# A graph-attention kernel whose GpSimd engine waits for finished sums at every fourth group of gathered rows instead of at every group

## The chip, the cores and the metric

The kernel runs on one core of a Trainium2 chip. The metric is the time of one execution on the device in microseconds (us). TensorE (PE) multiplies matrices, VectorE (DVE) and ScalarE (ACT) work elementwise, GpSimd (POOL) issues the gathers of rows, and SyncE (SP) issues the plain DMA transfers. The engines run their own instruction streams and meet at semaphores only.

## What is computed

A graph of 3,125 nodes with 256 features each goes through one layer: a layer norm, then x + graph attention + linear attention, then a second layer norm and a mixture of eight experts, of which every node uses two. The part that matters here is the graph attention over 53,125 edges (50,000 and a loop for each node), sorted by destination:

```
h = (x @ W).reshape(n, HEADS, C)
logits = a_src[src] + a_dst[dst]
logits = jnp.where(logits >= 0, logits, NEG_SLOPE * logits)
ex = jnp.exp(logits - seg_max[dst])
alpha = ex / (denom[dst] + 1e-16)
msgs = alpha[:, :, None] * h[src]
out = jax.ops.segment_sum(msgs, dst, num_segments=n)
```

The row `h[src]` of every edge has to be fetched from memory by an index, weighted, and added to the row of its destination.

## The kernel before

**Stages.** First all nodes are normalised and projected, and a table `h_table` with a row of 260 float32 for each node (256 features and 4 source logits) is written to memory. Then comes the edge loop, in which the linear attention and the second layer norm are worked in at fixed steps, and last the experts. The edges stand in 416 tiles of 128. Four tiles are a group (`G = 4`), so there are 104 groups (`NGRP`), numbered 0 to 103. The edge loop is written out group by group for every engine; on the inputs here it runs once.

**The ring.** The buffer `gathered` has eight places (`RING = 8`), and group `s` uses place `s % 8`. For each group GpSimd issues four indirect DMAs (L567), one for each tile: 128 rows of `h_table` picked by `src_row`. Place `r` may be overwritten once the sum that read it is finished. The semaphore `summed` says so: it starts at 8 and TensorE adds 1 at the end of each group's sum, so that the wait for `s + 1` before group `s` is a wait for the sum of group `s - 8`.

**A group's way.** TensorE spreads the destination's logits over the edges (`spread`, four products at L830, with some side work of `chain`: L855, L856, L861) and signals `ad_ready`. It does so three groups ahead. VectorE waits for the gather and for `ad_ready`, both before one instruction (`logits` part 0, L1161), finishes the logits (L1164, L1168), ScalarE takes the exponential (L681, L690), and VectorE weights the rows (`weigh`, L1173). TensorE then multiplies the rows by a one-hot matrix (the sum, four products at L887) and signals `summed`. VectorE adds the result to `acc` (`add_sums`, L1148). In the order of VectorE's code `weigh(n)` stands ahead of `logits(n + 2, part 0)`, and in TensorE's `spread(n + 3)` and `chain` stand ahead of the sum of group `n`:

```
                        if ahead >= 3:
                            last = spread(n + 3, s + 3, (r + 3) % RING)
                            last = chain(c, s + 3, last)
                            last.then_inc(ad_ready, 1)
                        pe.wait_ge(weighted, n + 1)
```

The trace has two matmul records for each float32 product, so 8 records at L887 are one group's sum and 8 at L830 one group's spread.

GpSimd does nothing else in this loop but wait, count and issue gathers. Two of its groups have another wait besides: group 3 for the copied keys and group 6 for the copied values of the linear attention.

Of the kernel before, what the change touches and what calls it, by code (L numbers as in the profile page):

```python
# [48 lines left out]
RING = 8  # L49
NGRP = ET // G  # L50
# [19 lines left out]
SLACK = 11  # L70
KGRP = -(-NT // G)
PLACES = 4
FAR = 3e38
EPS = 1e-5
SLOPE = 0.2
# [65 lines left out]
def graph_layer(nc, x, src, dst, w_gat, att_src, att_dst, gat_bias, w_qkv, w_out, b_out,  # L141
# [5 lines left out]
    with ExitStack() as whole:  # L147
        def sem(name):
            return whole.enter_context(nc.semaphore(name))
# [42 lines left out]
        waited = sem("waited")  # L192
# [6 lines left out]
        with ExitStack() as scope:  # L199
# [197 lines left out]
            summed = sem("summed")  # L397
# [15 lines left out]
            with nc.Block() as block:  # L413
# [86 lines left out]
                def _(pool):  # L500
# [54 lines left out]
                    with pool.Fori(0, passes) as c:  # L555
                        for s in range(NGRP):
                            r = s % RING

                            pool.wait_ge(summed, c * NGRP + s + 1)
                            pool.sem_inc(waited, 1)  # L560
                            if s == 3:
                                pool.wait_ge(k_copied, KGRP)
                            if s == 6:
                                pool.wait_ge(v_copied, KGRP)
                            for j in range(G):
                                t = s * G + j
                                pool.indirect_dma_start(gathered[:, r, j, :], None, h_table,  # L567
                                                        bass.IndirectOffsetOnAxis(ap=src_row[:, t:t + 1], axis=0)
                                                        ).then_inc(gather_done[r], 16)
# [794 lines left out]
        with ExitStack() as scope:  # L1364
# [13 lines left out]
            place, in_tile, what = [], [], []  # L1378
            for k in range(PLACES):
                at = k * sum(sizes)  # L1380
# [38 lines left out]
            with nc.Block() as block:  # L1419
# [26 lines left out]
                def _(pool):  # L1446
                    pool.memset(zeros[:, :], 0.0).then_inc(zeros_ready, 1)
                    for m in range(NCHOICE // UNROLL):
# [3 lines left out]
                        grid = (P, UNROLL, UT)  # L1452
                        pool.tensor_tensor(what[m % PLACES][:, :, 0, :], in_tile[m % PLACES],
                                           node_id[:, nodes].unsqueeze(2).broadcast_to(grid), ALU.mult).then_inc(what_ready, 1)

                @block.scalar
                def _(act):
                    act.wait_ge(ratio_ready, 1)
                    act.activation(ratio[:, :], ratio[:, :], ACT.Exp).then_inc(exp2_ready, 1)
                    for m in range(NCHOICE // UNROLL):  # L1460
                        act.wait_ge(tiles_found, m + 1)
                        for k in range(UNROLL):
                            n = m * UNROLL + k
                            op = act.activation(what[m % PLACES][:, k, 1, :], in_tile[m % PLACES][:, k, :], ACT.Copy,
                                                scale=share[:, n // NT, n % NT:n % NT + 1])
# [3 lines left out]
                def _(pe):  # L1469
# [11 lines left out]
                    for n in range(NCHOICE):  # L1481
# [3 lines left out]
                        m, k = n // UNROLL, n % UNROLL  # L1485
                        pe.matmul(bank[3][:, 0:2 * UT], place[m % PLACES][:, k, :],
                                  what[m % PLACES][:, k, :, :].rearrange("p a b -> p (a b)"),
                                  start=(n == 0), stop=(n == NCHOICE - 1)).then_inc(placed, 1)

                @block.vector  # L1490
                def _(dve):
                    def after(instruction):
                        v3.done(instruction)
                        dve.wait_ge(v3.sem, v3.n)
# [7 lines left out]
                    def choose(k):  # L1502

                        after(dve.tensor_reduce(best[:, k, :], gate[:, :, :], AX.X, ALU.max))
                        after(dve.tensor_tensor(ranked[:, :, :], gate[:, :, :], best[:, k, :].unsqueeze(2).broadcast_to(each), ALU.is_equal))
                        after(dve.tensor_tensor(ranked[:, :, :], ranked[:, :, :], by_rank, ALU.mult))
                        after(dve.tensor_reduce(first_rank[:, k, :], ranked[:, :, :], AX.X, ALU.max))
                        after(dve.tensor_tensor(choice[:, k * NT:(k + 1) * NT, :], by_rank,
                                                first_rank[:, k, :].unsqueeze(2).broadcast_to(each), ALU.is_equal))

                    choose(0)
                    after(dve.scalar_tensor_tensor(out=gate[:, :, :], in0=choice[:, 0:NT, :], scalar=-FAR, in1=gate[:, :, :],
                                                   op0=ALU.mult, op1=ALU.add))
# [34 lines left out]
                    def find(m):  # L1548
                        if m >= PLACES:

                            dve.wait_ge(placed, (m - PLACES + 1) * UNROLL)
                        some = slice(m * UNROLL, (m + 1) * UNROLL)
                        grid = (P, UNROLL, UT)
                        dve.tensor_tensor(in_tile[m % PLACES], tile_no[:, :].unsqueeze(1).broadcast_to(grid),
                                          slot_at[:, 1, some].unsqueeze(2).broadcast_to(grid), ALU.is_equal).then_inc(tiles_found, 1)
                        dve.tensor_tensor(place[m % PLACES], iota_row[:, :].unsqueeze(1).broadcast_to((P, UNROLL, P)),
                                          slot_at[:, 0, some].unsqueeze(2).broadcast_to((P, UNROLL, P)), ALU.is_equal).then_inc(places_ready, 1)
# [236 lines left out]
```

## Time and profile before

| what | value |
|---|---|
| median of 3 runs | 1165.52 us (1161.57 to 1167.33) |
| the profiled execution | 1165.62 us, span 1163.3 us |
| PE busy | 946.3 us, 81% of the span |
| DVE busy | 491.5 us, 42% |
| ACT busy | 397.3 us, 34% |
| POOL busy | 552.8 us, 48% |
| mean granted TensorE clock | 0.839 of full speed |

The profile is of one execution. Shares of busy time are averages over stages with different limits: the edge loop ends at about 708 us, and the rest of the span belongs to the experts. A PE record has a modelled end. An idle time in brackets is that of the engine just ahead of the instruction, with what ended it; "remote" is a semaphore whose sender the profile doesn't name, "issue" is no wait that the profile shows.

### The profile page before, as it was taken

What the parts mean: (1) busy time and instruction counts of PE and PEld (TensorE: products, weight loads), DVE (VectorE), ACT (ScalarE), POOL (GpSimd) and SP (SyncE); (2) the same over time, 40 slices, a digit from 0 to 9 for tenths busy, and PEclk for the clock granted to TensorE, in tenths of its full rate; (3) what the DMA queues carried; (4) which work ended last, traced back from release to release, by engine and by line L of the source; (5) the groups of instructions that cost most, each with busy time, mean ns of one, the idle gap of its engine ahead of it and who ended that gap; (6) DMA issues with size and microseconds to landing.
All of it is one profiled execution on the core that took longest, in us unless ns stands there. A gap on an engine that the chain in (4) does not pass through costs nothing. (4 is left out here: it accounts for less than half of the span.)

```text
span 1163.3 us, 18718 instructions
## 1 busy us (share of the span) xinstructions
PE 946.3 (81%) x5176; PEld 826.4 (71%) x5177; DVE 491.5 (42%) x1352; ACT 397.3 (34%) x1098; POOL 552.8 (48%) x572
## 2 busy tenths in 40 slices
PE   6949678687797888577568385599999999999995
PEld 5848656566675667466457373599999999999994
DVE  5754464555465466547457366711111111111110
ACT  4516332324233333333433222443333333333331
POOL 2263666666666666666566620423333333333332
PEclk8986977776877777777667677799999999999998
DMA  7342443444434444445444423956665655665661
GB/s 196 105 114 82 116 112 104 119 111 128 137 112 123 137 110 126 133 112 140 126 112 110 128 65 125 330 168 177 178 179 164 180 169 177 180 178 179 180 181 19
DMA packets 76350, 163.54 MB, mean 141 GB/s; under 512 B 11520, under 2 KB 40725, under 8 KB 76163
## 3 DMA queue, kind: packets, MB, share of 16 engines
q0 software_dynamic: 30144, 69.30, 24.7%
q1 hardware_dynamic: 45587, 93.02, 23.8%
q10 hardware_dynamic: 560, 0.52, 0.2%
q8 instruction: 25, 0.41, 0.1%
q14 instruction: 34, 0.28, 0.1%
HBM read 145.82 MB, written 16.99 MB: 140 GB/s over the span
## 5 line engine op out<-in xcount | busy, mean ns | idle before, releaser
L567 POOL DMA_INDIRECT gathered<-h_table,src_row x416 | 396.6, 953 | 233.6 <-issue 120.1
L887 PE MATMUL bank<-gathered,one_hot 128*128 128x260 f32 x832 | 281.3, 490 | 74.0 <-issue 43.1
L887 PEld LDWEIGHTS bank<-gathered,one_hot 128*128 128x128 f32 x832 | 192.3, 243 | 125.3 <-issue 90.2
L1676 ACT ACTIVATE hiddenT<-bank,b_slot 128x128 f32<-128x128 f32 x424 | 120.8, 368 | 248.6 <-PE bank L1711 248.5
L1654 POOL DMA_INDIRECT out<-y,add_index x53 | 84.4, 1593 | 248.2 <-DVE y L1766 122.5
L1711 PEld LDWEIGHTS bank<-xgT,acc 128*128 128x128 f32 x1696 | 198.5, 193 | 2.6
L1711 PE MATMUL bank<-xgT,acc 128*128 128x128 f32 x1696 | 198.7, 276 | 0.0
L1729 PE MATMUL bank<-w_sb,hiddenT 128*128 x848 | 193.2, 381 | 0.0
L830 PEld LDWEIGHTS bank<-adc,w_sb 128*128 128x128 f32 x832 | 138.7, 232 | 62.8 <-issue 52.2
L1729 PEld LDWEIGHTS bank<-w_sb,hiddenT 128*128 128x128 f32 x848 | 157.0, 190 | 21.7 <-issue 1.7
L830 PE MATMUL bank<-adc,w_sb 128*128 x832 | 123.0, 268 | 50.1 <-issue 49.8
L681 ACT ACTIVATE bank<-z 128x16 f32<-128x16 f32 x104 | 19.4, 187 | 390.4 <-DVE z L1168 339.7
L1173 DVE TENSOR_TENSOR gathered<-gathered,bank 128x1024 f32<-128x1024 f32 x104 | 126.1, 1213 | 0.9 <-ACT gathered L690 0.8
L1763 DVE CAST add_index<-slot_token 128x1 uint32 (+1 forms) x53 | 8.1, 154 | 279.6 <-PE bank L1729 279.6
L1161 DVE TENSOR_TENSOR z<-gathered,bank 128x16 f32<-128x16 f32 x104 | 17.4, 167 | 232.7 <-remote 201.5
L1148 DVE TENSOR_TENSOR acc<-acc,bank 64x260 f32 x208 | 87.8, 422 | 28.0 <-issue 23.1
L659 ACT ACTIVATE w_sb<-w_sb,minus_lane 128x512 f32<-128x512 int16 x104 | 74.8, 719 | 12.2 <-ACT w_sb L664 2.7
L664 ACT ACTIVATE w_sb<-w_sb,ones 128x512 f32<-128x512 f32 x104 | 73.7, 708 | 3.0 <-PE bank L830 2.7
L1136 DVE TENSOR_TENSOR one_hot<-bank,beyond 128x512 f32<-128x512 f32 x104 | 70.8, 684 | 0.4 <-issue 0.2
L1642 POOL DMA_INDIRECT xg<-xn_table,read_index x53 | 52.2, 985 | 22.4 <-issue 15.8
L855 PE MATMUL bank<-w_mix,xnT 128*128 128x256 f32 x100 | 36.9, 491 | 6.6 <-issue 6.4
L781 PE MATMUL bank<-w_sb,xnT 128*128 128x128 f32 x200 | 27.9, 303 | 7.1 <-ACT w_sb L621 5.6
(238 smaller groups left out, 697.1 us busy)
## 6 DMA issues: line engine op xcount, KB each, us to landing
acc<-in_L_ffn_W SPq DMA_DIRECT2D x53, 1024.0 KB
w_sb<-key_table SPq DMA_DIRECT2D x52, 256.0 KB
w_sb<-in_L_ffn_W SPq DMA_DIRECT2D x8, 1024.0 KB, 12.4
gathered<-h_table,src_row POOLq DMA_INDIRECT x416
h_table<-acc SPq DMA_DIRECT2D x25, 130.0 KB, 2.0
out<-w_sb SPq DMA_DIRECT2D x5, 512.0 KB
xn_table<-w_sb SPq DMA_DIRECT2D x5, 512.0 KB
xs<-in_x SPq DMA_DIRECT2D x3, 640.0 KB, 10.9
```

The costliest lines, as they stand in the source:

```text
L567: pool.indirect_dma_start(gathered[:, r, j, :], None, h_table, bass.IndirectOffsetOnAxis(ap=src_row[:, t:t + 1], axis=0)).then_inc(gather_ ...
L659: act.activation(key_offs, keys[:, q % KEYS, s % KBLK, :], ACT.Abs, bias=minus_lane[:, :]).then_inc(key_off, 1)
L664: act.activation(one_hotT[:, r % HOTS, :, :].rearrange("p a b -> p (a b)"), key_offs, ACT.Relu, bias=ones[:, 0:1], scale=-1.0).then_inc(ho ...
L830: mm = pe.matmul(ad_bank[r % ADS][:, j * 2 * HEADS:(j + 1) * 2 * HEADS], one_hotT[:, r % HOTS, j, :], flat(adc[:, bass.ds(k, 1), :]), star ...
L887: mm = pe.matmul(sum_bank[r % SUMS][:, 0:ROW], one_hot[:, r, j, :], gathered[:, r, j, :], start=(j == 0), stop=(j == G - 1))
L1136: dve.tensor_tensor(one_hot[:, r, :, :], lanes(place).unsqueeze(1).broadcast_to((P, G, P)), local[:, bass.ds(s * G, G)].unsqueeze(2).broad ...
L1148: dve.tensor_tensor(total, total, sum_bank[r % SUMS][part_of, 0:ROW], ALU.add).then_inc(added, 1)
L1173: dve.tensor_tensor(message, message, alpha(r).unsqueeze(3).broadcast_to((P, G, HEADS, C)), ALU.mult).then_inc(weighted, 1)
L1654: pool.indirect_dma_start(out, bass.IndirectOffsetOnAxis(ap=add_index[:, k:k + 1], axis=0), y[:, k, :], None, compute_op=ALU.add).then_inc ...
L1676: op = act.activation(hiddenT[:, k, g * P:(g + 1) * P], bank[1 + 2 * k + half][:, f * P:(f + 1) * P], ACT.Gelu, bias=b1_slot[:, k, g:g + 1])
L1711: mm = pe.matmul(bank[1 + 2 * k + f // 4][:, f % 4 * P:(f % 4 + 1) * P], w1_slot[:, k, c, f * P:(f + 1) * P], xgT[:, k, c * P:(c + 1) * P] ...
L1729: mm = pe.matmul(bank[5 + k][:, 0:D], hiddenT[:, k, f * P:(f + 1) * P], flat(w2_sb[:, bass.ds(e * KF + f, 1), :]), start=(f == 0), stop=(f ...
```

## The change

GpSimd no longer waits before each group. It waits before groups 0, 4, 8 and so on, and there for the sums of four groups at once: before group `s` for `s + 4`, which is for all sums up to that of group `s - 5`. It then issues the 16 gathers of groups `s` to `s + 3` with no wait for a sum between them. The count `waited` is raised as often as there are such waits. The other engines, the ring, and the gathers themselves are as before.

```diff
+HALF_RING = RING // 2
...
                         for s in range(NGRP):
                             r = s % RING
 
-                            pool.wait_ge(summed, c * NGRP + s + 1)
-                            pool.sem_inc(waited, 1)
+                            if s % HALF_RING == 0:
+                                pool.wait_ge(summed, c * NGRP + s + HALF_RING)
+                                pool.sem_inc(waited, 1)
                             if s == 3:
                                 pool.wait_ge(k_copied, KGRP)
```

In the instruction list of GpSimd, in the edge loop past group 7, the kernel before has a wait for `summed` at each fourth gather (the register operation is part of the loop's counting):

```order
L567 DMA gathered<-h_table,src_row 128x260 [waits summed]
L567 DMA gathered<-h_table,src_row 128x260 x3
L559 REGISTER_ALU
L567 DMA gathered<-h_table,src_row 128x260 [waits summed]
L567 DMA gathered<-h_table,src_row 128x260 x3
L559 REGISTER_ALU
```

At the same place of the changed kernel, where the gather's line is L569, and from group 4 on:

```order
L569 DMA gathered<-h_table,src_row 128x260 [waits summed]
L569 DMA gathered<-h_table,src_row 128x260 x7
L569 DMA gathered<-h_table,src_row 128x260 [waits v_copied]
L569 DMA gathered<-h_table,src_row 128x260 x7
L561 REGISTER_ALU
L569 DMA gathered<-h_table,src_row 128x260 [waits summed]
L569 DMA gathered<-h_table,src_row 128x260 x15
```

No gather has moved against another; what changes is that 16 of them now stand between two waits.

## Rows read from the trace of the kernel before

**Rows 1.** The page: the span, and the costliest groups of the edge loop

```profile
span 1163.3 us, 18718 instructions
...
L567 POOL DMA_INDIRECT gathered<-h_table,src_row x416 | 396.6, 953 | 233.6 <-issue 120.1
...
L1161 DVE TENSOR_TENSOR z<-gathered,bank 128x16 f32<-128x16 f32 x104 | 17.4, 167 | 232.7 <-remote 201.5
```

**Rows 2.** Windows, L887 alone: stretch, length, PE and PEld busy (count), PEclk, DMA, GB/s

```profile
52.00:125.00 73.00, 12.61 (x38) 9.34 (x39) 0.77 0.36 100
125.00:680.00 555.00, 254.82 (x747) 173.26 (x745) 0.75 0.44 121
680.00:708.50 28.50, 13.88 (x48) 9.72 (x48) 0.88 0.08 26
```

**Rows 3.** Line L567 by itself: ns of one, first and last start, idle before

```profile
L567 POOL DMA_INDIRECT gathered<-h_table,src_row x416: 940/946/1848, 51.8 to 678.7; - x139
...
  remote: 73.8, 23
  PE bank L887: 28.6, 11
```

**Rows 4.** Timeline 391 to 416 us: start, us busy, instruction, idle before

```profile
391.68 0.94 POOL L567 DMA_INDIRECT gathered<-h_table,src_row  x1 [3.17 <-PE bank L887]
...
400.63 0.41 PE L861 MATMUL bank<-ident,w_sb 128*128 128x128 f32 x2
...
400.88 1.92 PE L887 MATMUL bank<-gathered,one_hot 128*128 128x260 f32 x8
...
405.43 0.95 POOL L567 DMA_INDIRECT gathered<-h_table,src_row  x1 [0.30 <-issue]
...
408.75 0.17 DVE L1161 TENSOR_TENSOR z<-gathered,bank 128x16 f32<-128x16 f32 x1 [8.14 <-remote]
...
409.53 0.95 POOL L567 DMA_INDIRECT gathered<-h_table,src_row  x1 [3.15 <-PE bank L887]
...
412.15 3.83 PE L887 MATMUL bank<-gathered,one_hot 128*128 128x260 f32 x8 [2.06 <-DVE gathered L1173]
```

**Rows 5.** Groups by line, everything up to 402.9 us: counts

```profile
L567 POOL DMA_INDIRECT gathered<-h_table,src_row x229 | 218.1, 952 | 135.2 <-issue 65.5 <-remote 36.5 <-PE bank L887 22.0
...
L887 PE MATMUL bank<-gathered,one_hot 128*128 128x260 f32 x408 | 138.1, 490 | 29.6 <-issue 23.6 <-DVE gathered L1173 5.9
L830 PE MATMUL bank<-adc,w_sb 128*128 x436 | 65.1, 271 | 22.7 <-issue 22.5
...
L1161 DVE TENSOR_TENSOR z<-gathered,bank 128x16 f32<-128x16 f32 x53 | 8.9, 168 | 117.5 <-remote 100.2 <-PE bank L856 10.7 <-PE bank L830 4.2
```

**Rows 6.** Timeline 133 to 148.6 us, in the middle of 16 gathers

```profile
138.54 0.17 PE L830 MATMUL bank<-adc,w_sb 128*128 x1 [2.25 <-issue]
...
141.32 0.17 PE L830 MATMUL bank<-adc,w_sb 128*128 x1 [2.62 <-issue]
...
148.48 0.94 POOL L567 DMA_INDIRECT gathered<-h_table,src_row  x1 [3.77 <-remote]
```

**Rows 7.** Windows, L887 alone: six runs of 16 gathers, and one of 12

```profile
125.00:148.50 23.50, 6.65 (x27) 4.50 (x25) 0.84 0.39 103
202.10:225.60 23.50, 8.13 (x31) 5.18 (x29) 0.79 0.41 114
261.10:284.60 23.50, 12.63 (x32) 8.10 (x32) 0.72 0.48 136
350.30:373.80 23.50, 10.68 (x32) 6.93 (x32) 0.84 0.44 125
463.40:486.90 23.50, 8.42 (x31) 5.36 (x29) 0.83 0.48 136
540.10:563.60 23.50, 8.68 (x25) 5.76 (x24) 0.65 0.45 126
391.70:409.50 17.80, 8.36 (x24) 5.32 (x24) 0.76 0.40 105
```

## The prediction

> **What bounds the kernel now.** I read the page's groups first. GpSimd spends 396.6 us of its busy time on the 416 gathers and sits idle 233.6 us ahead of them; VectorE sits idle 232.7 us ahead of L1161, 201.5 of it for "remote" [rows 1]. So both ends of the ring wait for each other's chain. The windows of L887 give the loop's pace: between 125.0 and 680.0 us there are 747 records, 747 / 8 = 93.4 groups, 5.94 us each; in the last 28.5 us, when no gather is issued any more, 48 records, 6 groups, 4.75 us each [rows 2]. A gather takes 0.95 us [rows 3] and the next follows 0.30 us later [rows 4], so 1.25 us each and 5.0 us a group. Neither 4.75 nor 5.0 explains 5.94. The gathers' line names stalls of 73.8 us (23 times) and 28.6 us (11 times), 102.4 us or 3.0 us each [rows 3].
>
> The timeline shows what such a stall is. GpSimd starts at 391.68, the last of 12 gathers starts at 405.43 and ends at 406.38, and the next starts at 409.53: a period of 17.85 us for three groups [rows 4]. What is it waiting for? Count to 402.9: 408 records at L887 are 51 sums, groups 0 to 50 [rows 5]. GpSimd had issued 229 gathers by then [rows 5] and three more up to the stall, 58 groups, so it is at group 58, which needs the sum of group 50, whose products started at 400.88 and are modelled to end at 402.80 [rows 4]. Yet it goes on only at 409.53. VectorE has the same trouble: it has done L1161 53 times and wants `ad_ready` of group 53. The 54 spreads were dispatched by then (436 / 8 = 54.5 [rows 5]), with the side work over at 401.04, yet L1161 runs at 408.75 after 8.14 us of idling [rows 4]. The gather of group 53 can't be the reason, since it was issued four groups ahead of group 57. So TensorE's signals come some 6 us after the modelled end of the work, all together, and they come 2.4 us after the end of the last gather (406.38 to 408.75). In the middle of a longer run of gathers TensorE itself crawls: its records at L830 stand 2.8 us apart (138.54, 141.32) where eight of them otherwise take about 1 us, and GpSimd's stall ends at 148.48 [rows 6].
>
> My reading: while gathers follow one another without a break, TensorE's finished work is signalled for a few microseconds only; then the signals are held until the gathers have drained. GpSimd's short stalls, which look like a cost, are what lets the chain go on. The loop goes in periods: issue, drain (2.4 us), signals, restart 0.8 us later.
>
> **The change part by part.** *Waits and counts removed.* 78 waits and as many register operations go. GpSimd's 0.30 us between two gathers is the same with a wait between them or none, so this is worth nothing. *The place of the wait.* Group 8 now needs the sum of group 3, where it needed that of group 0. By 125.0 us 38 records, 4.75 sums, are dispatched [rows 2], and the first of the runs in [rows 7] starts there; I take 125.0 as the start of the refill of groups 8 to 11. *Longer runs.* From there each refill is 16 gathers in a row: 15 x 1.25 + 0.95 = 19.7 us, and then a pause. Queued behind the waiting gather are only the other 15 gathers of its refill; who waits for them is VectorE at L1161, four groups on at the earliest. Is a refill late for it? The first group of a refill has landed 4.7 + 2.4 = 7.1 us after the restart, and VectorE reaches it after `weigh` of two more groups; 0 to 3 us may be missing, and I take 0, since VectorE is then held by `ad_ready` longer than that.
>
> What decides is how many groups the chain gets through in one run of 16. The kernel before made six such runs, when its ring happened to have room: period 23.5 us each (19.7 and a pause of 3.8), with 27, 31, 32, 32, 31 and 25 sum records, 178 / 48 = 3.71 groups [rows 7]. A run of 12 carries 24 records, 3 groups, in 17.85 us. So a run that is a third longer carries less than a third more: 6.34 us a group against 5.95. Before, a missing 0.29 group only emptied the ring a little, and the next runs were shorter. Now the wait asks for all four. What is missing has to be done inside the pause. Its price: from the release at 408.75 to the end of the first new sum at 412.15 + 3.83 = 415.98 is 7.2 us [rows 4]. A group lacks in 0.29 of the periods: 0.29 x 7.2 = 2.1 us, and the period is 23.5 + 2.1 = 25.6 us. Bounds: no group ever lacks, and the pause is the short one of 3.15 us: 22.85 us. One lacks every time: 30.7 us. I stay near the six measured runs, which are the only rows with this very pattern.
>
> *The end.* The last gather before ends at 679.65, 28.85 us ahead of 708.5, with 6 sums to go. After the last refill, 96 + 3.7 sums are done and 4.3 are to go: 4.3 x 4.75 + 0.35 = 20.8 us.
>
> *The sum.* 24 refills: 125.0 + 23 x 25.6 + 19.7 + 20.8 = 754.3 us against 708.5, so +45.8 us. The experts behind the loop start later and are otherwise the same. Against the profiled execution, 1165.6 (span 1163.3 and 2.3 around it), that gives 1211 us; it stands 0.1 us from the median of 1165.5, so nothing is to be corrected. One microsecond of the period is worth 23 us.
>
> **Against a rule of the skill.** That gathers hold back TensorE is my inference from the rows. The Trainium skill, page "SBUF — State Buffer", section "Who interferes with whom", says the contrary: a DMA never contends with a compute engine. By that rule the release at 408.75 would have its cause elsewhere and a longer run would hold nothing longer. That is the first rival below; the trace, with a release 2.4 us behind the last gather [rows 4], doesn't agree with it as far as I can see.
>
> **The rivals.**
> 1. *The held signals have nothing to do with the gathers.* TensorE's chain sets its own beat of 5.95 us a group, and GpSimd, with 20 us of work in 23.8, follows it. Then 125.0 + 23 x 23.8 + 40.5 = 712.9, +4.4 us: 1170 us. For it: the ring has four groups in stock when a refill starts. Against it: in the stretch without gathers the beat is 4.75, and a release behind the drain. This is also what comes out if a refill carries nearly four groups (period 23.5: 1163 us).
> 2. *Faster: fewer stops.* If every refill carries four groups, the pauses of 3 us come 24 times instead of some 32. Period 22.85: 691.1, -17.4 us: 1148 us. For it: four of the six runs of 16 have 31 or 32 records, so four groups can be done. Against it: those runs had a sum in progress at the restart, which the new wait lets happen less often. It decides from a period under 23.3 us.
> 3. *A group lacks every time.* TensorE carries three groups in a run however long it is. Period 30.7: 871.6, +163 us: 1329 us. Against it: only two of the six runs carried as few as 25 or 27 records; and a pause in which the signals run freely puts the chain ahead, so that the next refill starts better.
>
> **How the numbers follow.** The forecast has a chance of 0.54, rival 1 has 0.19, rival 2 has 0.16, rival 3 and what lies toward it 0.11. The likeliest one's own range: a group lacks in one period of six (24.7 us, 1191 us) to one in two (27.1 us, 1246 us). The range over all takes in rival 1 and reaches to rival 2: 1148 to 1252 us. A measurement of this kernel tells about 0.5%, 6 us, from no change: faster 0.16, within it 0.19, slower 0.65.
>
> **What the changed kernel's profile would show.** GpSimd's line has about 24 long idle times past group 8 instead of 34 in all [rows 3], of 4 to 11 us each and 6 on average. From about 125 us on its runs are of exactly 16 gathers. VectorE's idle time ahead of L1161 grows by some 45 us. Each run of 16 shows L1161 waiting until 2.4 us after its last gather. The loop ends near 754 us, and the stretch of the experts keeps its 455 us. I am wrong if the pauses stay near 3 us, if TensorE signals all through a run of 16, or if the first refill starts far from 125 us.

## The result, and the profile after

The changed kernel takes 1218.28 us (median of 4 runs, 1207.74 to 1225.71), the kernel before 1163.55 us on the same chip (4 runs, 1160.76 to 1167.33). The ratio is 1.0476, 95% interval 1.0439 to 1.0512: slower by 55 us. The profiled execution took 1221.62 us, its span 1219.3 us; that is the one read here.

The experiments ran on other chips of the same type, and these are of two kinds. On some the kernel before takes 1162 to 1172 us as above (I call them chips that hold, after the first theory below; the name doesn't say that the theory is shown); on others, called quick below, it takes 1043 to 1045 us. So each experiment is compared only with the kernel before on its own chip, and of each I say which kind it was.

The page of the changed kernel, the rows that answer to [rows 1]:

```profile
span 1219.3 us, 18562 instructions
...
L569 POOL DMA_INDIRECT gathered<-h_table,src_row x416 | 396.8, 954 | 296.8 <-PE bank L889 143.2
L889 PE MATMUL bank<-gathered,one_hot 128*128 128x260 f32 x832 | 298.2, 505 | 97.1 <-issue 74.8
...
L1163 DVE TENSOR_TENSOR z<-gathered,bank 128x16 f32<-128x16 f32 x104 | 17.4, 167 | 288.4 <-remote 241.2
```

The gathers cost what they did (396.8 us of busy time against 396.6). GpSimd's idle time ahead of them grew by 63.2 us, VectorE's ahead of the logits by 55.7 us. Both ends of the ring wait longer, as they did before, for the chain between them. The gathers' line by itself, as in [rows 3]:

```profile
L569 POOL DMA_INDIRECT gathered<-h_table,src_row x416: 941/947/1872, 52.0 to 742.1; - x139
...
  PE bank L889: 143.2, 20
...
  remote: 15.8, 4
```

34 stalls of 3.0 us have become 24 stalls of 6.6 us (159.0 / 24): fewer and over twice as long. The windows of the sum's line, with the columns of [rows 2]: ahead of the first refill with the new wait, from it to the start of the last one, and the end; then two single periods:

```profile
52.00:123.60 71.60, 9.27 (x33) 6.96 (x34) 0.79 0.30 86
123.60:723.20 599.60, 266.62 (x736) 175.89 (x736) 0.71 0.40 110
723.20:766.00 42.80, 22.32 (x64) 15.24 (x64) 0.70 0.28 81
...
388.06:414.15 26.09, 9.99 (x32) 6.81 (x32) 0.80 0.44 122
414.15:442.36 28.21, 9.69 (x32) 6.84 (x32) 0.76 0.40 118
```

Group 8 starts at 123.6 us and group 100 at 723.2 us: 23 periods of 599.6 / 23 = 26.07 us, each with 736 / 23 = 32 records, four sums. The pace was 5.94 us a group [rows 2] and is now 6.52 us. In every period GpSimd issues 16 gathers, twice with a gap of under 2 us inside. What one period looks like, in the timeline from 386 to 416 us:

```profile
388.06 0.95 POOL L569 DMA_INDIRECT gathered<-h_table,src_row  x1 [11.54 <-PE bank L889]
...
396.14 2.02 PE L889 MATMUL bank<-gathered,one_hot 128*128 128x260 f32 x8 [0.66 <-issue]
...
400.11 0.18 PEld L858 LDWEIGHTS bank<-w_sb,ones 1*128 1x128 f32 x1 [0.61 <-issue]
...
406.40 0.59 PE L889 MATMUL bank<-gathered,one_hot 128*128 128x260 f32 x1 [1.52 <-issue]
406.86 0.95 POOL L569 DMA_INDIRECT gathered<-h_table,src_row  x1 [0.31 <-issue]
409.20 0.59 PE L889 MATMUL bank<-gathered,one_hot 128*128 128x260 f32 x1 [2.21 <-issue]
410.60 2.76 PE L889 MATMUL bank<-gathered,one_hot 128*128 128x260 f32 x6 [0.81 <-issue]
410.75 0.17 DVE L1163 TENSOR_TENSOR z<-gathered,bank 128x16 f32<-128x16 f32 x1 [11.53 <-remote]
...
414.15 0.94 POOL L569 DMA_INDIRECT gathered<-h_table,src_row  x1 [6.34 <-PE bank L889]
```

The last gather of the run ends at 406.86 + 0.95 = 407.81 us. TensorE isn't slow through the whole run: three of the four sums (at 388.24, 392.67 and 396.14) take 2.02 us each, with gathers being issued beside them. From the weight load at 400.11 us, 12 us into the run, its weight loads and products come one at a time, 1.40 us apart. Up to the end of the run, and a little beyond, the records of the sum stand alone, 2.8 us apart (406.40, 409.20), as those at L830 in [rows 6]. At 410.60 six come in one piece, and at 410.75, 2.94 us behind the end of the gathers, VectorE gets a signal for which it idled 11.53 us. Then the rest of the sum is finished, GpSimd is released at 414.15 and the next 16 gathers begin. Over all 23 periods the pause is between 3.5 and 11.5 us.

The loop ends at 765.8 us, against 708.3 us in the profiled execution of before: +57.5 us. The experts behind it take 453.5 us (it was 455.0). So the whole difference of the spans, 56.0 us, is made in the edge loop.

### The profile page after: what moved, and what is told of

Its sections match the earlier page's. It is cut to its first block and busy times, and to the rows that moved or that the text cites. A ratio compares the mean times of both kernels' runs of the same rounds, so it can differ in the third digit from the quotient of the medians.

```text
span 1219.3 us, 18562 instructions
## 1 busy us (share of the span) xinstructions
PE 969.5 (80%) x5176; PEld 838.5 (69%) x5177; DVE 491.9 (40%) x1352; ACT 397.7 (33%) x1098; POOL 553.1 (45%) x572
## 5 line engine op out<-in xcount | busy, mean ns | idle before, releaser
L569 POOL DMA_INDIRECT gathered<-h_table,src_row x416 | 396.8, 954 | 296.8 <-PE bank L889 143.2
L889 PE MATMUL bank<-gathered,one_hot 128*128 128x260 f32 x832 | 298.2, 505 | 97.1 <-issue 74.8
L889 PEld LDWEIGHTS bank<-gathered,one_hot 128*128 128x128 f32 x832 | 198.1, 249 | 165.5 <-issue 131.5
L1731 PEld LDWEIGHTS bank<-w_sb,hiddenT 128*128 128x128 f32 x848 | 157.0, 190 | 20.8 <-issue 0.7
L832 PE MATMUL bank<-adc,w_sb 128*128 x832 | 125.7, 272 | 46.3 <-issue 42.7
L1163 DVE TENSOR_TENSOR z<-gathered,bank 128x16 f32<-128x16 f32 x104 | 17.4, 167 | 288.4 <-remote 241.2
L857 PEld LDWEIGHTS bank<-w_mix,xnT 128*128 128x128 f32 x100 | 21.9, 238 | 25.7 <-issue 23.7
```

The source lines that it names most:

```text
L832: mm = pe.matmul(ad_bank[r % ADS][:, j * 2 * HEADS:(j + 1) * 2 * HEADS], one_hotT[:, r % HOTS, j, :], flat(adc[:, bass.ds(k, 1), :]), star ...
L889: mm = pe.matmul(sum_bank[r % SUMS][:, 0:ROW], one_hot[:, r, j, :], gathered[:, r, j, :], start=(j == 0), stop=(j == G - 1))
L1731: mm = pe.matmul(bank[5 + k][:, 0:D], hiddenT[:, k, f * P:(f + 1) * P], flat(w2_sb[:, bass.ds(e * KF + f, 1), :]), start=(f == 0), stop=(f ...
```

## The experiments

Two theories were to be told apart. **Held:** while gathers follow one another without a break, TensorE's finished work is signalled late, and the long runs cost time because of it. **Own beat:** TensorE's chain has a beat of some 6 us a group of its own, and the changed kernel is slow because its refill asks for sums up to group `s - 5`, so that only four groups are in stock when it starts, and the chain runs dry. Each edit is against the kernel before unless it says otherwise; where only the wait is changed its count `waited` stays with it. Where an expectation gives times in us for chips that hold and the run met a quick one, its numbers can't be tested by that run.

**1. Halves of a half: a wait at every second group (e1).** A quick chip.

```diff
-                            pool.wait_ge(summed, c * NGRP + s + 1)
-                            pool.sem_inc(waited, 1)
+                            if s % 2 == 0:
+                                pool.wait_ge(summed, c * NGRP + s + 2)
+                                pool.sem_inc(waited, 1)
```

> GpSimd waits at every second group, for the sums up to two groups on (so for that of group s - 6). Held-signal theory (TensorE's finished signals are held while gathers follow one another, and come when the gathers have drained): runs of 8 or 16 gathers, a run of 8 takes 9.7 us and a pause of 3.1 for at most two groups (6.4 us a group), one of 16 takes 23.5 for four (5.9); the time lies between the two kernels, 1170 to 1195 us, I take 1180. Own-beat theory (TensorE's late signals have nothing to do with gathers; the change costs because the ring is asked for a later sum, so that GpSimd starts with too little in stock): also between, 1180 to 1190, with no mark in the length of the runs. This run gives the slope and doesn't tell the two apart.

Measured: 1046.17 us against 1044.0, 1.0021 (1.0002 to 1.004). The gathers' line of this kernel by itself:

```profile
L568 POOL DMA_INDIRECT gathered<-h_table,src_row x416: 942/946/1914, 51.4 to 573.9; - x139
...
  issue: 126.7, 409
  PE bank L888: 3.3, 7
...
  DVE z L1162: 125.9, 90
```

Seven stalls with 3.3 us in all. Past 93.09 us the gathers run to the end of the loop without a pause, and VectorE waits for the gathers (the last row: who waited for this line), not for TensorE. Here GpSimd's 1.25 us a gather is the bound, and nothing is held. The run tells nothing on the change, but it shows that the stalls of [rows 3] don't belong to the kernel's code alone: nearly the same code has none here.

**2. The smaller stock without the long wait (e2, e7, e9).** Each group asks for the sum of group `s - 5`, as the changed kernel's refills do, but one group at a time. Three quick chips.

```diff
-                            pool.wait_ge(summed, c * NGRP + s + 1)
+                            pool.wait_ge(summed, c * NGRP + s + RING // 2)
```

> GpSimd waits at every group as in the kernel before, but always for the sum of group s - 5, as the changed kernel does at its fourth groups: the ring has the smaller stock of the changed kernel throughout, and the stops of the kernel before. Held-signal theory: the stops come as soon as a sum is missing, the gathers drain after about 12, and the chain goes on; near the kernel before, 1160 to 1180 us. Own-beat theory: the stock is what costs, so at least as slow as the changed kernel, 1215 to 1240 us.

> The short lead again (wait at every group, for the sum of group s - 5), for a chip on which the kernel before takes about 1164 us; the ones met so far take 1043 to 1045. On a chip that holds signals: the held-signal theory says near the kernel before, ratio 0.995 to 1.015; the own-beat theory says as slow as the changed kernel or slower, 1.045 to 1.07. On one that doesn't: as in the first run of this kernel, 1.010, from the start of the loop alone.

> The wait at every group for the sum of group s - 5, once more for a chip that holds signals (kernel before 1164 to 1169 us). There: held-signal theory, the same sums are asked for as by the changed kernel, but GpSimd stops at the first that is missing and drains, so runs of about 12 gathers and a ratio of 0.995 to 1.015; own-beat theory, the asked-for sum is what costs, 1.045 to 1.07. On a chip that doesn't hold them, 1.010 to 1.015 as twice before.

Measured: 1054.89 us against 1044.0, 1.0102 (1.007 to 1.0135); 1059.04 against 1043.04, 1.0151 (1.0096 to 1.0206); 1055.43 against 1042.85, 1.0129 (1.0101 to 1.0157). The gathers' line in the first of them, and the longest of its stalls, from the timeline:

```profile
L567 POOL DMA_INDIRECT gathered<-h_table,src_row x416: 942/946/1846, 51.4 to 585.9; - x139
...
  PE bank L887: 23.0, 32
```

```profile
89.96 0.94 POOL L567 DMA_INDIRECT gathered<-h_table,src_row  x1 [13.54 <-PE bank L887]
```

13.54 of the 23.0 us are at group 5, when the pipeline has not yet filled; the 31 others come to 9.5 us, 0.3 us each, no more than the step between any two gathers. So what a smaller stock costs here is a late start.

**3. Stops in the middle of a run (e3, e10, e4).** In the changed kernel GpSimd also waits, at the third group of each refill, until the group before has landed; in e4 the kernel before does so at every third group. The first edit below is that of e3 and e10, against the changed kernel, and is meant to shorten its runs to eight gathers; the second is that of e4.

```diff
+                            if s % HALF_RING == 2:
+                                pool.wait_ge(gather_done[(s - 1) % RING], ...)
+                                pool.sem_inc(waited, 1)
```

```diff
+                            if s > 0 and s % 3 == 0:
+                                pool.wait_ge(gather_done[(s - 1) % RING], ...)
+                                pool.sem_inc(waited, 1)
```

> The changed kernel, and in the middle of each refill (before group s + 2) GpSimd waits for its own gathers of group s + 1 to land, 2.4 us. Held-signal theory: the signals are let out in mid-refill, so the pause at the end of the refill shrinks from 6.3 us on average to about 3.3, which pays for the stop; period 25 to 26 us, 1195 to 1220 us. Own-beat theory: the stop is added to the rest, period 28.5 us, 23 x 2.4 = +55 us, about 1270 us.

> The changed kernel with a stop of GpSimd for its own gathers in the middle of each refill. On a chip that holds signals: held-signal theory, the pause behind a refill shrinks from 6.3 to about 3.3 us, which pays for the stop, ratio to the kernel before 1.03 to 1.05; own-beat theory, the stop is added, 1.09 to 1.10. On a chip that doesn't hold them, 1.06 as before (1109.9 against 1044.0 us).

> The kernel before, and ahead of every third group GpSimd also waits for its own gathers of the group before to land. Held-signal theory: the gathers are then made to drain each 12 of them, with a restart at the landing and not 0.8 us after the signal; period 14.7 + 2.5 + 0.1 = 17.3 us for three groups against 17.85, at best 16 us less: 1148 to 1168 us, the runs of 16 are gone. Own-beat theory: the stops are either hidden (1164 us) or, where GpSimd has no time to spare, cost up to 2.4 us each.

Measured, all three on quick chips: 1109.91 us against 1044.0, 1.0621 (1.0595 to 1.0648); 1109.07 against 1042.85, 1.0635 (1.0603 to 1.0666); and e4 1135.66 against 1044.0, 1.088 (1.0853 to 1.0907). The stalls of e3, and those of e4:

```profile
L572 POOL DMA_INDIRECT gathered<-h_table,src_row x416: 940/946/1902, 52.0 to 639.6; - x139
...
  DMA gathered<-h_table,src_row: 66.9, 25
```

```profile
L570 POOL DMA_INDIRECT gathered<-h_table,src_row x416: 940/946/1967, 51.5 to 664.8; - x139
...
  DMA gathered<-h_table,src_row: 74.4, 25
  PE bank L890: 24.0, 13
```

In e3 25 stops of 2.7 us make 66.9 us, and the kernel is 65.9 us slower. Here GpSimd is the bound, and a stop costs its whole length. What I had expected of e4, no more than a small loss, was worked out for a chip that holds; on this one it missed by far. How such stops do on a chip that holds wasn't measured.

**4. The changed kernel on a quick chip (e5).** No edit.

> The changed kernel again, on another chip than the one of the first comparison. The four kernels run so far met a chip on which the kernel before takes 1044 us instead of 1164, with gathers back to back from 93 to 575 us and no held signals. On such a chip the held-signal theory says the refills have nothing to stop for: GpSimd leaves the start some 8 us later (group 8 waits for sum 3) and then issues without a pause, 1.00 to 1.012 of the kernel before. Own-beat theory (the asked-for sum is what costs, signals or not): pauses behind each refill here too, 1.03 to 1.06. On a chip that holds signals both say 1.04 to 1.055 and a period of 26 us.

Measured: 1050.23 us against 1045.13, 1.0054 (1.0032 to 1.0077). Its gathers' line, a window of the sum's line, and the first stall of a refill in GpSimd's timeline:

```profile
L569 POOL DMA_INDIRECT gathered<-h_table,src_row x416: 942/946/1866, 51.0 to 584.1; - x139
...
  issue: 125.7, 406
  PE bank L889: 13.1, 10
```

```profile
101.60:585.00 483.40, 261.44 (x772) 180.56 (x773) 0.80 0.51 142
```

```profile
101.63 0.95 POOL L569 DMA_INDIRECT gathered<-h_table,src_row  x1 [10.40 <-PE bank L889]
```

The same kernel, the same waits, and no pause of a refill but the first: 384 gathers run back to back. The windows give 772 / 8 = 96.5 sums in 483.4 us, 5.0 us each. The chain of TensorE keeps up with GpSimd, the waits for four sums at once find them done. What is left is the late start: group 8 goes at 101.63 us, where e1 had it at 93.09. (The 8.5 us between them are more than the 5.1 us by which the medians differ; the profiled execution of e5, 1056.9 us, is the slowest of its eight.) So a beat of 6 us doesn't belong to the code of TensorE's chain; whether it belongs to the chips that hold, this run can't say.

**5. A still smaller stock (e6).** Each group asks for the sum of group `s - 4`. A quick chip.

```diff
-                            pool.wait_ge(summed, c * NGRP + s + 1)
+                            pool.wait_ge(summed, c * NGRP + s + 5)
```

> GpSimd waits at every group, for the sum of group s - 4: half of the ring is in use at most, a stock smaller than the changed kernel's, but a wait at each group. On a chip that holds TensorE's signals: the held-signal theory says the gathers stop whenever a sum is missing and drain there, so it must come out clearly under the changed kernel, 1160 to 1195 us; the own-beat theory says the smaller stock makes it slower than the changed kernel, over 1220. On a chip that doesn't hold them both say: from sum (7 us to issue and land four gathers, some 9 us to the sum) a group's place comes free in 16.5 us for four groups, under GpSimd's 20, so no pauses in the middle, only a start with 16 gathers less in stock, +15 to +22 us, 1.015 to 1.021.

Measured: 1095.73 us against 1042.94, 1.0506 (1.0475 to 1.0538), three times what was expected. The gathers' line:

```profile
L567 POOL DMA_INDIRECT gathered<-h_table,src_row x416: 940/946/1681, 51.6 to 629.9; - x139
...
  PE bank L887: 66.4, 42
...
  DVE z L1161: 185.2, 96
```

42 stalls, all through the loop. With places for four groups GpSimd has to stop for the chain in the middle of the loop too; with five (e2) it hardly has to. The expectation had put a place's way round at 16.5 us for four groups, under GpSimd's 20, and so forecast no such stops: that was wrong. So the theory of the own beat has a point: the stock matters, but only one group further down than the changed kernel goes.

**6. Late halves (e8).** The changed kernel, but up to group 11 the waits are those of before, so that it doesn't start late. A chip that holds.

```diff
-                            if s % HALF_RING == 0:
+                            if s < 12:
+                                pool.wait_ge(summed, c * NGRP + s + 1)
+                                pool.sem_inc(waited, 1)
+                            elif s % HALF_RING == 0:
                                 pool.wait_ge(summed, c * NGRP + s + HALF_RING)
                                 pool.sem_inc(waited, 1)
```

> The changed kernel, but groups 0 to 11 keep the wait of the kernel before (for the sum of group s - 8), and the refills in halves begin at group 12. On a chip that doesn't hold signals the changed kernel's 0.5% lay in GpSimd's late start at group 8 (101.6 us instead of 93.1, 8.5 us, with no pause behind it). If that is all, this kernel takes at most 2 us more than the kernel before, ratio 0.998 to 1.003, and has at most one pause past group 8, at group 12. If the halves cost something in each refill as well, 1.005 or more. On a chip that holds signals: 1.04 to 1.05, since there the price is paid in each refill.

Measured: 1230.06 us against 1168.77, 1.0526 (1.0482 to 1.057), a little above what was expected for such a chip. The gathers' line:

```profile
L572 POOL DMA_INDIRECT gathered<-h_table,src_row x416: 943/949/1583, 52.5 to 748.9; - x139
...
  PE bank L892: 144.7, 20
...
  remote: 21.6, 6
```

26 stalls with 166.3 us. What fills such a pause stands in its timeline:

```profile
401.61 0.17 DVE L1166 TENSOR_TENSOR z<-gathered,bank 128x16 f32<-128x16 f32 x1 [8.93 <-remote]
...
402.56 0.95 POOL L572 DMA_INDIRECT gathered<-h_table,src_row  x1 [0.30 <-issue]
...
406.76 0.17 DVE L1166 TENSOR_TENSOR z<-gathered,bank 128x16 f32<-128x16 f32 x1 [1.84 <-remote]
...
408.99 3.84 PE L892 MATMUL bank<-gathered,one_hot 128*128 128x260 f32 x8
...
413.62 0.95 POOL L572 DMA_INDIRECT gathered<-h_table,src_row  x1 [10.11 <-PE bank L892]
```

The run ends at 403.51 us, the signals come at 406.76, and a whole sum (408.99 to 412.83) is still to be done before GpSimd goes on at 413.62: the group that lacks, as the prediction priced it. Group 12 starts at 140.10 us and group 100 at 729.68 us: 22 periods of 26.8 us. The loss is there in full, so it isn't the start but the periods.

**7. Each sum asked for by itself from group 12 on (e11, e12).** The wait of e2 with the start of before. It and e8 need, at the start of a refill, the very same sum. Inside a refill e8 asks for nothing more, while e11 asks for one more sum ahead of each further group: it asks for all that e8 asks for, and more, and GpSimd may stop inside the refill. A chip that holds, twice (another one than e8's).

```diff
-                            pool.wait_ge(summed, c * NGRP + s + 1)
+                            pool.wait_ge(summed, c * NGRP + s + (1 if s < 12 else RING // 2))
```

> Groups 0 to 11 keep the wait of the kernel before; from group 12 on GpSimd waits at every group, for the sum of group s - 5. It asks for the same sums as the kernel with late halves, but stops at the first that is missing. On a chip that holds signals, where the late halves took 1.053 of the kernel before: held-signal theory 0.995 to 1.015, own-beat theory 1.04 or more. On a chip that doesn't hold them: the short lead's 1.010 to 1.015 lay in the late start at group 5, so 0.998 to 1.004 here if the stock itself costs nothing; if it does, 1.006 or more.

> The late short lead again, to see on what its 0.9935 depends. On a chip that holds signals it should repeat, 0.990 to 0.998: shorter runs of gathers, so more frequent releases. On one that doesn't hold them there is nothing to release: 0.998 to 1.004 if the short lead's 1.010 to 1.015 lay in the start of the loop, 1.006 or more if the smaller stock costs by itself.

Measured: 1165.68 us against 1171.91, 0.9935 (0.9903 to 0.9966), a little below the 0.995 that was expected, and 1151.79 against 1161.75, 0.9925 (0.99 to 0.995). The gathers' line of e11, and a stretch of its timeline:

```profile
L567 POOL DMA_INDIRECT gathered<-h_table,src_row x416: 943/949/1618, 51.9 to 693.0; - x139
...
  PE bank L887: 61.7, 22
  remote: 58.2, 18
```

```profile
377.46 0.95 POOL L567 DMA_INDIRECT gathered<-h_table,src_row  x1 [3.35 <-PE bank L887]
...
391.25 0.95 POOL L567 DMA_INDIRECT gathered<-h_table,src_row  x1 [0.30 <-issue]
...
394.89 0.17 DVE L1161 TENSOR_TENSOR z<-gathered,bank 128x16 f32<-128x16 f32 x1 [5.85 <-PE bank L861]
395.66 0.95 POOL L567 DMA_INDIRECT gathered<-h_table,src_row  x1 [3.47 <-remote]
```

40 stalls of 3.0 us (119.9 / 40), more than the 34 of before [rows 3], and yet the kernel isn't slower: it is the only one here that beats the kernel before on its chip, by 0.7%. Most of its runs are 12 gathers long. The one shown ends at 391.25 + 0.95 = 392.20 us, VectorE's signal comes 2.7 us later and GpSimd goes on after 3.47 us; the pauses lie between 2.5 and 4.1 us. In e8, with the same demand at the start of a refill, a stall is 6.4 us in the mean (166.3 / 26). That is the change's cost, isolated to the form of the wait: +61 us with the wait for four sums at once, -6 and -10 us with a wait for each.

On the quick chips the same short stock with an early start costs 1.0 to 1.5% (e2, e7, e9). The late form wasn't run there, so whether it beats both kernels everywhere is open. Where its gain of 0.7% on the chip that holds comes from isn't located either: the loop ends at 708.3 us in e11's profiled execution and at 694.7 in e12's, that of before ended at 708.3 on another chip, and there is no trace of before on theirs.

## Why the prediction came out as it did

The forecast was 1211 us, slower; it measured 1218.28 us, and the way it went is the one described.

- **Removed waits, worth nothing:** right. The median gather is 0.947 us and the next follows 0.30 us later, as before.
- **Start of the first refill:** 125.0 forecast, 123.6 measured, -1.4 us.
- **Length of a run:** 16 gathers between two pauses, as forecast, but 19.95 us in the mean instead of 19.7: most take 19.7, three take 21.1 to 21.3, with a gather that took longer or a gap of 1.7 us inside.
- **The period:** 25.6 us forecast, 26.07 measured. This is the term that was mis-sized. Over 23 periods the 0.47 us make +10.8 us, the larger part of what the forecast lacked. About half of it is the longer run (19.95 for 19.7), the other half the pause: 6.12 us in the mean instead of 5.9. The pause's two parts were both off, and their errors nearly cancel, which is luck. Of the 23 pauses, 15 last 3.5 to 6.3 us, 4.5 in the mean, where the forecast had 3.8; eight last 7.2 to 11.5, 9.2 in the mean. If those eight are the periods in which a group lacks, that is one in three (0.35, forecast 0.29) and 4.8 us more each, not 7.2.
- **The end:** 20.8 us from the last gather forecast, 22.8 measured (743.0 to 765.8), +2.0 us. -1.4, +10.8 and +2.0 give +11.4 us on the loop's end, forecast at 754.3 and found at 765.8.
- **Signals for a few microseconds, then none until the drain:** so it looks in the run that began at 388.06 us. VectorE ran L1163 at 388.02, 392.46 and 395.92 us, and then not before 410.75.
- **VectorE's idle time ahead of the logits:** +45 forecast, +55.7 measured, by the same excess.
- **Release 2.4 us after the last gather of a run:** 1.6 to 3.2 us measured, 2.9 in the median of the 23 pauses.
- **The experts' stretch:** 455 forecast, 453.5 measured.

**Rival 1, the signals have nothing to do with the gathers.** Its time, 1170 us, didn't come: a beat of its own gives a period of 23.8 us, and 26.07 were measured. Against its mechanism speaks that TensorE's chain does 5.0 us a group on a quick chip (e5), and that on chips that hold e8 and e11, with the same stock at the start of a refill, differ by 6% with the length of the runs of gathers. Nor does the chain run dry: when VectorE at last runs L1163 at 410.75 us, the last gather of that group (49) had been issued at 396.83, 13.9 us earlier. Of VectorE's 41 waits of over 2 us ahead of that line in the whole loop only eight, 26 of 285 us, end within 5 us of the issue of their group's last gather. The Trainium skill, page "SBUF — State Buffer", section "Who interferes with whom", says that a DMA never contends with a compute engine. On the quick chips the trace agrees: 142 GB/s are moved in e5's window beside sums at full pace. On the chips that hold the trace looks otherwise: TensorE's records stand 2.8 us apart late in the run, and six come at once 2.8 us behind its last gather; what makes them so isn't shown. It isn't a plain contention for memory, which every chip would show.

**Rival 2, faster by fewer stops.** There were fewer, 24 for 34, and they were worth nothing, since what has to be done in them grew. Its point of decision, a period under 23.3 us, was missed by 2.8 us. **Rival 3, a group lacks every time** (period 30.7, so a pause of 11.0), happens in some periods, as the pause of 11.54 us shows, but not in all.

**What is shown and what is argued.** Shown: the loss lies in the periods and not in the start (e8), it goes when GpSimd may stop inside a refill though it asks for no fewer sums (e11, e12), and it shrinks to 0.5% on a chip whose traces have no late signals (e5). Argued: that back-to-back gathers are what holds the signals. It rests on the time between a run's last gather and VectorE's next L1163 (or its like): over the pauses of more than 2 us past the first refills it is in the median 2.4 us in before, 2.9 in the changed kernel, 3.1 in e8 and 2.6 in e11, and in each of the four only three or four are shorter than that by more than 1 us. No run took the gathers away from such a chip or put a forced stop there. And not every signal waits for the end: in e8 VectorE gets one at 401.61 us, in the middle of a run, after 8.93 us of idling, and the next at 406.76, 3.25 us behind its last gather.

What in those chips holds the signals is open. It isn't that the gathers themselves are slower: from the start of a gather to the end of its last DMA packet pass 2.4 to 2.5 us in the median, 4.3 to 4.6 at most, in the traces of both kinds (before, after, e8, e11, e12; e1, e5). One trait goes with the kind: the traces of chips that hold contain 7,372 to 7,622 records of semaphore updates, those of the quick chips 14,427 to 14,542, for nearly the same program. Outside the edge loop the two have the same number, 4,925 to 4,964; inside it 2,436 to 2,679 stand against 9,481 to 9,583, and of the 416 x 16 = 6,656 updates by which the gathers report their landing 1,035 to 1,221 are left, against 6,640 to 6,651. So records are missing in the very stage where the signals are late. A rival that no run tests follows from it: on these chips the updates of the gathers, or the recording of them, may be what delays the other signals, and not the moving of data. The granted clock of every execution here was read from such a recording, so whether a run without one would be held, and whether the change would cost 5% there, isn't known.

## What to carry to other kernels

A wait that takes a whole batch of buffers at once turns many short stops into few long ones, and the long ones cost more where, as on the chips that hold, a consumer gets on mainly in the stops: look in the timeline at what the other engines do in a stall before counting it as lost. Where the ring is asked to keep a smaller stock, ask at every group and not for a batch (e11 against e8), and find out how small the stock may be by one run with it smaller (e6: four groups 5%, five groups 1 to 1.5%). Compare with the old kernel on the same chip each time; between chips the same program differed by 12% here, and an edit that costs 5% on one cost 0.5% on another.

## What was not expected of the hardware

The same kernel takes 1043 to 1045 us on five chips (e1 to e7, e9, e10) and 1162 to 1172 us in the first comparison and on the two chips of e8 and of e11 and e12, nothing between. The difference is all in the edge loop: it ends at 586.9 us in e1, whose code is nearly that of before, and at 708.3 us in [rows 4]'s execution, 121 us apart, as the medians are (1163.55 - 1044.0 = 120). On the quick chips that loop is bound by GpSimd: 0.946 us a gather and 0.30 us to the next, with 4 x 1.25 = 5.0 us a group and no pause but at the first refills. The granted TensorE clock isn't the same: 0.80 of full speed in the window of e5, 0.71 over the 23 periods of the changed kernel. But it explains little of the difference: the mean product of the sum takes 362 ns there (266.62 / 736) against 339 in e5 (261.44 / 772), 17 us over the 736, where the loops end 168 us apart (765.8 and 598.0), and in the period from 388.06 to 414.15 us the clock is 0.80, as in e5, with 26.09 us for four sums.
